# A conditioned transformer block on one core: the MLP's products as seven block products, all stages feature-major

## The reference

```
rmsnorm(x, w) = x * rsqrt(mean(x * x) + 1e-6) * w
film(x, cond, w, b): ss = cond @ w + b; scale, shift = split(ss); x * (1 + scale) + shift
h = film(rmsnorm(x, norm1_w), cond, film1_w, film1_b)
Q, K, V = h @ q_w + q_b, h @ k_w + k_b, h @ v_w + v_b
attn = softmax(Q K^T * D ** -0.5)              # within each batch of 128 tokens
x = x + attn @ V @ proj_w + proj_b
h = film(rmsnorm(x, norm2_w), cond, film2_w, film2_b)
out = x + gelu(h @ mlp_w1 + mlp_b1) @ mlp_w2 + mlp_b2
```

## Time and profile before

| | |
|---|---|
| median of 3 runs | 1961.46 us (1957.05 to 1961.47) |
| profiled execution | 1959.93 us |
| its span, first to last instruction | 1958.1 us |
| mean granted TensorE clock | 0.996 |
| busy: PE, PEld | 1935.4, 1591.2 us |
| busy: DVE, ACT, POOL | 684.7, 679.5, 345.0 us |
| DMA | 120.32 MB, mean 61 GB/s |

### The profile page before, as it was taken

One profiled execution on the slowest core, in us unless ns is written; L12 is line 12 of the kernel. 1 busy time (PEld: TensorE's weight loads), 2 busy tenths in 40 slices (PEclk: granted clock), 3 DMA queues, 4 the chain that ended last, 5 costly groups with the idle time before them and its releaser, 6 DMA issues.

```text
span 1958.1 us, 23715 instructions
## 1 busy us (share of the span) xinstructions
PE 1935.4 (99%) x8806; PEld 1591.2 (81%) x8806; DVE 684.7 (35%) x1206; ACT 679.5 (35%) x1387; POOL 345.0 (18%) x354
## 2 busy tenths in 40 slices
PE   9989999999899999999999999999999999999999
PEld 8777887878678888888888888888888888888887
DVE  6655546455544222322222232222222232222211
ACT  4334434444343333333233233233333333333322
POOL 1442433424364010110101010110101011010100
PEclk9999999999999999999999999999999999999999
DMA  8323132231431101101010101101010110101000
GB/s 304 118 76 130 68 125 101 92 129 65 139 108 54 52 13 54 54 14 51 21 46 18 54 29 35 54 19 46 21 52 12 54 54 13 51 21 46 19 22 22
DMA packets 86923, 120.32 MB, mean 61 GB/s; under 512 B 13664, under 2 KB 39264, under 8 KB 86880
## 3 DMA queue, kind: packets, MB, share of 16 engines
q1 hardware_dynamic: 86880, 119.75, 19.1%
HBM read 70.41 MB, written 33.55 MB: 53 GB/s over the span
## 4 chain that ended last, share of the span: by engine, by line
PE 95%; DVE 3%; ACT 1%; issue 0%; DMA 0%; SPq 0%; POOL 0%; DVEq 0%; ACTq 0%; POOLq 0%
PE score L467 21%; PE pT L467 18%; PE ring L643 12%; PE ring L644 12%; PE ring L647 12%; PE ring L467 10%; PE ring L550 3%; PE ring L549 3%; PE ring L553 3%; DVE h L828 2%; PE ring L504 1%; DVE xT_in L820 1%; PE pT L582 0%; DMA wkT<-wkT_dram 0%; DVE wqT L916 0%
## 5 line engine op out<-in xcount | busy, mean ns | idle before, releaser
L1037 DVE TENSOR_TENSOR act_lo<-act_full,act_hi 128x512 fp32r<-128x512 f32 x256 | 189.9, 742 | 969.3 <-ACT act_full L770 969.3
L643 PE MATMUL ring<-w_hi,act_hi 128*128 128x512 f32 x1020 | 396.8, 389 | 0.0
L644 PE MATMUL ring<-w_lo,act_hi 128*128 128x512 f32 x1020 | 396.8, 389 | 0.0
L647 PE MATMUL ring<-w_hi,act_lo 128*128 128x512 f32 x1020 | 272.6, 389 | 0.0
L769 ACT ACTIVATE act_hi<-score,vecs 128x512 fp32r<-128x512 f32 x128 | 88.3, 690 | 481.8 <-PE score L467 481.8
L769 ACT ACTIVATE act_hi<-pT,vecs 128x512 fp32r<-128x512 f32 x128 | 88.3, 690 | 457.5 <-PE pT L467 457.4
L647 PEld LDWEIGHTS ring<-w_hi,act_lo 128*128 128x128 f32 x1020 | 191.5, 188 | 39.8
L644 PEld LDWEIGHTS ring<-w_lo,act_hi 128*128 128x128 f32 x1020 | 191.5, 188 | 39.7
L643 PEld LDWEIGHTS ring<-w_hi,act_hi 128*128 128x128 f32 x1020 | 191.5, 188 | 39.7
L467 PE MATMUL score<-h_hi,w_hi 128*128 128x512 f32 x512 | 199.6, 390 | 0.0
L467 PE MATMUL score<-h_lo,w_hi 128*128 128x512 f32 x512 | 199.2, 389 | 0.0
(11 more groups left out here) (136 smaller groups left out, 2712.4 us busy)
## 6 DMA issues: line engine op xcount, KB each, us to landing
x_in<-x_dram SPq DMA_DIRECT2D x64, 256.0 KB, 3.5
xT_in<-xT_dram SPq DMA_DIRECT2D x16, 1024.0 KB, 7.3
x_scratch<-x_in SPq DMA_DIRECT2D x64, 256.0 KB, 2.1
x_in<-x_scratch SPq DMA_DIRECT2D x64, 256.0 KB, 3.5
out_dram<-x_in SPq DMA_DIRECT2D x64, 256.0 KB, 2.2
h_half<-blocks SPq DMA_DIRECT2D x480, 32.0 KB, 1.9
stage<-w_dram SPq DMA_DIRECT2D x32, 256.0 KB, 2.7
f2w<-f2w_dram SPq DMA_DIRECT2D x1, 2048.0 KB, 15.6
```

The costliest lines, as they stand in the source:

```text
L643: pe.matmul(ring[b][:], act_hi[r][:, tokens(b)], w2_hi[:, j, :], start=j == 0, stop=False)
L644: pe.matmul(ring[b][:], act_hi[r][:, tokens(b)], w2_lo[:, j, :], start=False, stop=False)
L647: mm = pe.matmul(ring[b][:], act_lo[r][:, tokens(b)], w2_hi[:, j, :], start=False, stop=j == KH - 1)
L1037: dve.tensor_tensor(act_lo[r][:], act_full[r][:], act_hi[r][:].bitcast(F32), ALU.subtract).then_inc(act_lo_done[r], 1)
```

## The change

Nearly the whole kernel is rewritten. Its parts:

- **MLP by block products.** Tokens are taken in pairs of groups (1024), and features, hidden units and tokens are each cut in two halves. A product of 2x2 blocks is made of seven block products (Strassen's scheme in Winograd's form) instead of eight, both for up and for down. Each still is three fp32r products.
- **Weights.** Each block product has its own weight block or sum of blocks. POOL makes the sums and their hi and lo in attention groups 1 to 8 (`sum_weights`, `split_weights`: 8 chunks of 4 sums and 7 splits, 128x512 each) and SP stores them in DRAM (wu, wd). In the MLP they are streamed back for every pair, 112 slots of 128x512 (256 KB), through a ring of 8.
- **Operands.** For h of the next pair: DVE makes four sums of 1024 columns (`mix_t1`, `mix_t2_to_t4`), ACT seven hi, DVE seven lo (1024 columns each). For the hidden activations the 28 stages of the down phase each take `stage_high` (ACT) and `stage_low` (DVE) of 1024 columns, and DVE makes the sums x_t1 (`turn_12`) to x_t4 in place.
- **Joins.** The seven results are added on DVE out of PSUM (`join_up` five a step, `join_down` twelve a pair); three blocks accumulate in a bank that holds another block product already, after that one was read. POOL adds six 128x512 blocks to the residual (`add_residual`). gelu is now evaluated once per tile.
- **Feature-major.** x and h have features on the partitions everywhere. Norm factors: ACT squares, sums over features by PE (`sum_features`) in the MLP or by token tiles in attention, through DRAM into a row that is broadcast to all partitions; DVE multiplies by it (`scale_x`, `scale_pair`). DVE transposes, the block moves and `spread_rstd` are gone. `output` has v stationary and pT_sb moving: 16 products of 128 columns. Probabilities are scaled by 1/den before they are transposed.
- **Order.** All 16 attention groups and 8 MLP pairs are straight code. In attention, `scale_x` and the modulation of the next group stand ahead of the wait for the scores; g(n+1) is interleaved with output(n). The folded weights are loaded first; film 2 is computed in group 1. The first pair's operands are made in attention groups 9 to 15.

```diff
+RING = 8
+SLOTS = 56
+UP_ORDER = ("P1", "P6", "P7", "P5", "P2", "P4", "P3")
+DOWN_ORDER = ("P1", "P5", "P6", "P7", "P2", "P4", "P3")
+SPLIT_ORDER = ("P6", "P7", "P4", "P1", "P5", "P2", "P3")
+BANK = {"P1": 0, "P2": 0, "P6": 1, "P7": 2, "P4": 2, "P5": 3, "P3": 3}
+FRESH = ("P1", "P6", "P7", "P5")
...
 # SP, MLP
+            for p in range(PAIRS):
+                for i in range(SLOTS):
+                    if p > 0 or i >= RING:
+                        load_slot(stream(p, 0, i))
...
+                for i in range(SLOTS):
+                    load_slot(stream(p, 1, i))
+                    if i == 18:
...
+                        sp.dma_start(xres[:], x2T_chunks[:, :, PAIR * p:PAIR * p + PAIR]).then_inc(xres_loaded, 16)
+                    if i == 52:
+                        if 2 <= p + 2 < PAIRS:
+                            load_hn(p + 2)
+                        store_out(p, 1, 1, down_c22, 2 * p + 2)
...
 # PE, MLP
+            def sum_features(m, squares, into):
+
+                pe.wait_ge(sq_added, 3 * m + 3)
+                for b in range(2 * GB):
+                    mm = pe.matmul(into[:, b:b + 1], squares[:, 0, tokens(b)], ones_r[:, 0:1].bitcast(F32),
+                                   start=True, stop=True)
+                mm.then_inc(stat_full, 1)
...
+                pe.wait_ge(slot_loaded[w % RING], 16 * (w // RING + 1))
+                a, to = ring[w % RING], bank(q, s)
+                steps = [t for kt in range(2) for t in split3(a[:, kt, 0, :], a[:, kt, 1, :],
+                                                              op_hi[q][:, kt, :], op_lo[q][:, kt, :])]
...
+            for p in range(PAIRS):
+                for jj in range(HALF):
+                    for q in UP_ORDER:
...
+                        up(p, jj, q)
+                        if q == "P2" and jj == 1 and p < PAIRS - 1:
+                            pe.wait_ge(gelu11, HALF * p + 1)
+                            sum_features(p + 1, sq_mlp, ps[0])
+                for q in DOWN_ORDER:
+                    for ss in range(4):
+                        down(p, q, ss)
...
 # ACT, MLP, step jj
+                    act.wait_ge(slot_done, up_slot(p, jj, "P1"))
...
+                    nc.scalar.copy(p1_copy[:, s, :], bank("P1", s)[:]).then_inc(up_p1_copied, 1)
+                    if jj > 0:
+                        gelu_12(p, jj - 1)
+                    if jj == HALF - 1:
+                        stage_high(28 * p)
+                        stage_high(28 * p + 1)
+                    act.wait_ge(up_c22, at_step)
+                    gelu(gelu22, x22, jj, x22[:, jj, :], HALF + jj)
+                    if jj == 0 and p < PAIRS - 1:
+                        squares_of_pair(p + 1, sq_mlp)
+                    act.wait_ge(slot_done, up_slot(p, jj, "P2"))
+                    gelu(gelu11, x11, jj, bank("P2", s)[:], jj)
+                    act.wait_ge(up_c21, at_step)
+                    gelu(gelu21, x21, jj, x21[:, jj, :], HALF + jj)
...
 # DVE, MLP, step jj, after join_up of u2, v and c22
+                    if jj > 0:
+                        turn_12(p, jj - 1)
+                    more = p < PAIRS - 1
+                    if jj == 1 and more:
+                        add_squares(p + 1, sq_mlp)
+                    if jj == 4 and more:
+                        scale_pair(p + 1)
...
+                    if jj == 7:
+                        if more:
+                            mix_t1(p + 1)
+                        stage_low(28 * p)
+                        stage_low(28 * p + 1)
...
 # DVE, down phase, stage k
+                    if k < 26:
+                        stage_low(28 * p + k + 2)
+                    if k == 0:
+                        turn_12(p, HALF - 1)
+                    if 2 <= k < 6:
+                        turn(x_t2, x12, x22, x12, k - 2, x_t1, HALF * p + 2 * (k - 2) + 2)
+                    if 6 <= k < 10:
+                        turn(x_t3, x11, x12, x11, k - 6, x_t2, 4 * p + k - 5)
+                    if k in (10, 12, 13, 14):
+                        ss = (10, 12, 13, 14).index(k)
+                        turn(x_t4, x12, x21, x12, ss, x_t3, 4 * p + ss + 1)
+                    if k in (0, 1, 2, 16, 17, 20, 21) and more:
+                        operand_low(p + 1, SPLIT_ORDER[(0, 1, 2, 16, 17, 20, 21).index(k)])
```

More of the change, by code:

```diff
@@ new lines, in cond_block_kernel @@
+        slot_loaded, slot_done = sems("slot_loaded", RING), sem("slot_done")
+        up_p1_copied, up_u2, up_v, up_c22, up_c21, up_c12 = (
+            sem("up_" + n) for n in ("p1_copied", "u2", "v", "c22", "c21", "c12"))
+        gelu11, gelu12, gelu21, gelu22 = (sem(n) for n in ("gelu11", "gelu12", "gelu21", "gelu22"))
+        x_t1, x_t2, x_t3, x_t4 = (sem(n) for n in ("x_t1", "x_t2", "x_t3", "x_t4"))
+        hi_done, hi_used, lo_done = sem("hi_done"), sem("hi_used"), sem("lo_done")
+        down_p1_copied, down_u2, down_v, down_c22, down_c11, down_c21, down_c12 = (
+            sem("down_" + n) for n in ("p1_copied", "u2", "v", "c22", "c11", "c21", "c12"))
@@ L694, in h_high_mlp @@
[L694 to L712 removed]
+                    at_b = h[m % 2][:, k, tokens(b)]
@@ L718, in keep_v @@
[L718 to L729 removed]
+                nc.scalar.copy(hi[:, c, :], gv[c][:]).then_inc(prod_hi[c], 1)
@@ new lines, in stage_high @@
+            def stage_high(st):
+                p, i, ss = st // 28, st % 28 // 4, st % 4
+                q = DOWN_ORDER[i]
+                if st >= 2:
+                    act.wait_ge(hi_used, st - 1)
+                    act.wait_ge(lo_done, st - 1)
+                ready, count = {"P1": (gelu11, 2), "P5": (x_t1, 2), "P6": (x_t2, 1), "P7": (x_t3, 1), "P2": (gelu21, 2),
+                                "P4": (x_t4, 1), "P3": (gelu22, 2)}[q]
+                act.wait_ge(ready, count * (4 * p + ss + 1))
+                nc.scalar.copy(stage_hi[st % 2][:], down_source[q][:, 2 * ss:2 * ss + 2, :]).then_inc(hi_done, 1)
@@ new lines, in _ @@
+                if n == 1:
+                    film_coefs(1, film2, "f2b", "n2")
+                if n == 10:
+                    add_squares(0, sq_attn)
+                if n == 12:
+                    scale_pair(0)
+                if n == 13:
+                    dve.wait_ge(film_read, 2)
+                    modulate_pair(0, 0)
+                    modulate_pair(0, 1)
+                    mix_t1(0)
+                    mix_t2_to_t4(0)
+                if n == 14:
+                    for q in SPLIT_ORDER[:3]:
+                        operand_low(0, q)
@@ new lines, in _, with join_up, turn_12 @@
+                if n == LAST:
+                    for q in SPLIT_ORDER[3:]:
+                        operand_low(0, q)
+                add_output(n, 0)
+                add_output(n, 1)
+                if n == 10:
+                    keep_sums(0, pT)
+            add_output(LAST, 2)
+            add_output(LAST, 3)
+            def join_up(sem_done, into, q, s, other):
+                dve.tensor_tensor(into, bank(q, s)[:], other[:, s, :], ALU.add).then_inc(sem_done, 1)
+            def turn_12(p, jj):
+                dve.wait_ge(gelu12, HALF * p + jj + 1)
+                dve.wait_ge(gelu11, HALF * p + jj + 1)
+                dve.tensor_tensor(x12[:, jj, :], x12[:, jj, :], x11[:, jj, :], ALU.subtract).then_inc(x_t1, 1)
```

1592 lines of the change are left out of this document (817 added, 775 removed).

## The result

The changed kernel takes 1971.1 us (median of 4, 1968.15 to 1974.15) against 1960.41 (1957.05 to 1961.47) for the kernel before on the same chip: ratio 1.0053, 95% interval 1.0038 to 1.0069. It is slower by half a per cent; the forecast was 1886. The profiled execution has a span of 1966.4 us, 83.9 more than the sum's 1882.5.

The account below looks back on a forecast made before the run. The tensor engine, busy 99% of the span, was taken as the bound. MLP start 566.6, plus products 1218.7, losses 41.3, 19.6, 12, 8, 11 and tail 5.3, gave span 1882.5 and forecast 1886 us, range 1865 to 1910.

Parts of the forecast that it names:

- start of g(0): Setup: weights loaded first and one film gone, so g(0) starts at 42.5 us instead of 47.5.
- g(0) to the MLP's start: Attention: groups 496.8 us, film 2 7.7, delays in later groups 13.6, weight splitting 6; MLP starts at 566.6.
- up and down products: MLP: 5376 products instead of 6144 at 0.2267 us each, 1218.7 us.
- stop, sums of squares, clock: MLP up phase: 3.7 us wait for add_squares, 5.9 with sums, in 7 pairs, 41.3 us; clock falls add 19.6.
- scale_pair: MLP up phase: reading the norm row at every eighth word delays the joins, 0 to 17 us, taken as 8.
- down phase lateness: MLP down phase: residual additions slow VectorE, stages 16 to 19 run late, 1.5 us a pair, 12 in all.
- stream: MLP weight ring: rate fits, but hn load and a store delay slot 53; 11 us, bounds 0 and 45.
- The rival of weight splitting: Attention: eight groups lose 8 us each to GpSimd's weight splitting, 1950 us; chance 0.09.
- the 8 of the rival: MLP down phase: the vector engine bounds it, 8 us a pair instead of 1.5, 1938 us; chance 0.13.
- the signs named: Whole kernel: 3 to 4 us gap with half clock, stage_lo waits below 2 a pair, slot waits near hn, groups 31 us.
- a stream that does not keep its rate: MLP weight ring: a slot takes longer than 1.36 us; at 1.5 it costs 125 us and gives 2011; chance 0.10.
- mishaps that add up: Whole kernel: several losses together, subtracted without a size of their own from the 0.88 chance of being faster.

Follow-up runs that it names:

- e1: Changed kernel with the sums of squares moved from step 1 to step 2 of the up phase: 1917.5 us, ratio 0.9791.
- g2: As g1, with ScalarE copying the norm row once into batch order so VectorE's scale operations read it densely: 1823.77 us, ratio 0.9309.
- g1: As f4, but with the norm row stored as in the changed kernel, read at every eighth word: 1848.43 us, ratio 0.9439.
- e3: Changed kernel with GpSimd's six residual additions per pair left out: 1943.12 us, ratio 0.9924.
- e4: Changed kernel with the 2 MB load of hn split into four loads of 512 KB: 1950.05 us, ratio 0.9948.
- h1: Changed kernel with the 96 one-column records of its setup cut to 6: 1959.12 us, ratio 1.0005.
- e2: Changed kernel with a second buffer for the weights' source chunks, the next loaded during splitting: 1951.44 us, ratio 0.9957.
- f3: Changed kernel with residual additions moved from GpSimd to VectorE's slack stages and the last block's store moved to the next pair: 1932.43 us, ratio 0.9864.
- f4: Changed kernel with e1, e2, e4, f2, f3, a densely stored norm row, chunk 1 loaded earlier, pair 0's squares and modulation split: 1857.69 us, ratio 0.9483.
- f2: Changed kernel with 64 one-column setup records moved from ahead of the film products to between the second weight products: 1971.36 us, ratio 1.0066.
- h2: As g2, with the last two squares of pair 0 done singly at separate places in group 10: 1819.08 us, ratio 0.9304.

## Why the prediction was wrong

The forecast was faster by 4%, and the kernel is slower by half a per cent. The saving that it rests on was right and its largest term exact (5376 products at 0.2267); what failed is the sum of the losses around it, which was put 84 us too low. Us of the span, or of the ratio where an experiment gives it:

| step | predicted | measured | by |
|---|---|---|---|
| start of g(0) | 42.5 | 61.4 | timeline |
| g(0) to the MLP's start | 524.1 | 546 | D-phase start of pair 0 (696.4) less 88.9 |
| up and down products | 1218.7 | 1218.6 | last up phase, 16 times |
| stop, sums of squares, clock | 60.9 | 64 | 51 (e1) and 7 x 1.84 left |
| scale_pair | 8 | 25 | g2 against g1 |
| down phase lateness | 12 | 25 | e3 |
| stream | 11 | 21 | e4 |
| both together | 23 | 46 | down phases over 76.2 each |

The steps that failed, in the order of the kernel:

- **"First product near 7 ..., g(0) at 42.5"**, 18.9 us. The first product is at 7.37. The sum left out the three column products, which the new kernel has and the trace of before does not show: 96 records, 11.0 us at the earlier trace rows's 0.115. The first 64 of them and the film products make a stretch of 23.5 us without a wait, in which the clock falls after 4 us, and the film takes 13.7 us where the earlier trace rows would give 7.4. h1 shows both: without the columns the film takes 7.3 and g starts at 44.5. The term of the clock was thought of in the MLP alone.
- **"GpSimd splits weights in groups 1 to 8 ... 0.75 each, 6"**, 22 us. Groups 2 to 8 together are 28.5 us longer than at 30.3 each. The rival of weight splitting had the right place, but as contention; it is a serial loop through one buffer and one queue (7.9 us of store issues, the load behind them, 14 us without work for GpSimd), and e2 takes it away at the same GpSimd work. SP's order had been read for the MLP's ring, and not for this. Groups 9 and 13 are 11.8 and 6.0 long over 30.3 where 2.1 and 4.5 were taken; in group 9 the same queue had a part. On the other side a group costs 30.3, not 31.05, which gives 12 us back over sixteen. The attention term as a whole is 22 us out.
- **scale_pair: "0 to 17 us, I take 8"**, 17 us. An operation takes 2.13 us instead of 1.22, near the upper bound's "twice as slow", and the stop itself is 7 times 1.85, 13 us, inside the range; the value of 8 was a middle between bounds, although the strided read had no row for being cheap. The range left out what follows the stop, the lower clock or the string of small hand-overs, another 12 us.
- **"makes stages 16 to 19 0.2 to 0.5 late. I take 1.5 a pair"** for the down phase, 13 us. What a residual addition does to a subtraction was right: 1.09 us (2.31 against 1.22), predicted 1.1. So was the price of a subtraction: they start 1.14 apart, predicted 1.15. What was off is the slack that they meet: four of the six additions fall on the same two stages, where 4.4 us are lost against 1.95 of lead and 0.45 a stage. TensorE waits 1.41 in stage 16 and 0.62 in stage 19, 2 us a pair, and e3 gives back 3 (0.7 of it waits for slots), between the 1.5 of the forecast and the 8 of the rival.
- **"1 to 1.5 us late, in six pairs"**, 10 us: they are 1.9 to 2.8. The load of hn and a store stand together ahead of slot 53. e4 cuts the load, in f3 the store has moved, and each of the two takes these waits down to 0.6 us or less.

Right were the stop of 3.65 us in seven pairs, its clock (3.4 with the slower sums, 2.8 taken), and the rate of the stream (no slot waits outside the two bursts). Of the signs named, the gap with the lower clock and the place of the slot waits came true (but for two short ones near the load of xres); the waits for stage_lo are 2.1 us a pair, not below 2, and groups 2 to 8 take 31 to 37 us, not 31. The chance of 0.10 for slower was given to one mechanism, a stream that does not keep its rate, which did not happen. The slower kernel came of six terms that each missed upward: +19, +22, +17, +13, +10 and +3 make the 84 us. That they close to the microsecond is luck, as three of them come from experiments good to 4 us, and e3 and e4 overlap (f3, which has neither loss, saves 37, not 46, and leaves 8 us in the down phases that no edit explains). But the phases of the trace say the same: +19 in the setup, +22 in attention, +20 in the up and +23 in the down phases. The rivals were thought through one at a time, and the sum of them was put at "mishaps that add up".

The lock of the Trainium skill ("SBUF — State Buffer", section "SBUF: two separate sides") was weighed in the prediction. Its picture, in which the loser waits out the other's whole instruction, roughly fits the trace: GpSimd's addition and VectorE's subtraction keep step, one of each in 2.24 us, where alone they start 1.24 (the weight sums of the same shape) and 1.14 us apart. The price that the prediction drew from it, 1.5 us an addition, doesn't: it is 1.09. So the "near 24" that stands with it meets the 25 of e3 by luck, all the more as 6 of the 25 are waits for slots.

## What to carry to other kernels

A change that takes 9% of the work off a full engine leaves every other engine and queue that much less cover, so each must be laid out against the new pace: what stands in TensorE's queue ahead of a slow helper, two bursts in one DMA queue, a helper engine that slows the vector engine in its tightest stages. Move a wait to where its producer has long finished before touching anything else: sums one step later gave 51 us, additions moved to slack stages 37 together with a store moved out of a burst. List every instruction that the new code adds, the small ones of the setup too, and where several terms are open on the same side, give their joint miss a chance of its own.

## What the runs showed of the hardware

- In the changed kernel the granted clock fell at or just behind all seven stops of 3.65 us and behind four of the seven of 1.85; in f4 it fell behind a stop of 3.19 us between full products. Sixteen one-column records in full work (e1, 1.84 us) did not bring it down. In the setup it fell 4 us into a run of one-column records, and again within 1.5 us of the end of the last 32 of them (3.5 us), without a stop; 64 records of 64 columns (h1 and f2, 7.3 us) ran at full clock.
- An fp32 operand read at every eighth word makes a VectorE operation of 1024 columns take 2.13 us instead of 1.22. ScalarE's copy of the same row in g2 costs the path nothing.
- VectorE (1024 columns) and GpSimd (512), both with two SBUF inputs: 1.22 and 1.28 us alone, 2.31 and 2.21 together.
- A store of 1024 single words takes 13.1 us to land instead of 2.9, and 256 KB loads in the same queue take 11.7 instead of 3.0.

Open: in the four versions that fill the second source buffer at the end of group 1 (f4, g1, g2, h2), group 2 takes 38.7 to 40.4 us, while groups 3 to 8, with the vector engine and GpSimd at the same work, take 30.3 to 31.0. In h2 eight modulation operations of group 2 take 9.0 us, those of the later groups 3.1. In e2, which fills it later, group 2 takes 30.5 and group 3 43.3. That wasn't tried further.
